# A windowed-attention block on one core: the rows for the MLP are transposed on VectorE and through device memory, not on TensorE; the batch loops get a prefetch hint

## The reference, cut to what matters

```python
xs = jnp.roll(x, shift=(-4, -4), axis=(1, 2))          # then cut into windows of 64 tokens
h = _ln(win, ln1_g, ln1_b)
q, k, v = (einsum('ntc,chd->nthd', h, w) + b for each of the three)
attn = softmax(einsum('nqhd,nkhd->nhqk', q, k) / sqrt(32), axis=-1)
win = win + einsum('nhqk,nkhd->nqhd', attn, v) @ wo + bo
h2 = _ln(win, ln2_g, ln2_b)
win = win + gelu(h2 @ w1 + b1, approximate=False) @ w2 + b2     # w1: 96 x 384, w2: 384 x 96
```

## Time and profile before

| what | value |
|---|---|
| median of three runs | 5434.65 us (5433.81 to 5440.99) |
| the profiled execution | 5443.81 us, its span 5442.0 us |
| busy: PE, DVE, ACT, POOL | 95%, 77%, 69%, 57% of the span |
| mean granted TensorE clock | 0.987 |
| DMA | 208.20 MB on SP's queue, 13.0% of 16 engines |
| device memory | 107.45 MB read, 100.66 MB written |

### The profile page before, as it was taken

How to read it: one execution, slowest core, us unless ns; L and a number is a source line. 1 busy time by engine, 2 the same in 40 slices (tenths; PEclk the granted TensorE clock), 3 DMA queues, 4 the chain that set the end, 5 groups by cost and what they waited for, 6 DMA issues and landing times.

```text
span 5442.0 us, 275140 instructions
## 1 busy us (share of the span) xinstructions
PE 5176.5 (95%) x105172; PEld 4395.4 (81%) x105172; DVE 4179.8 (77%) x9862; ACT 3741.6 (69%) x7758; POOL 3083.7 (57%) x3053
## 2 busy tenths in 40 slices
PE   6999999999999999999999999999999999999999
PEld 4887888878788787888878888788887888878888
DVE  6968768687686877869778697786977869688696
ACT  6839568495784957749477594875938659396693
POOL 5645646466464655646556466464664646556464
PEclk8999999999999999999999999999999999999999
DMA  3011020110201102010120201202011020110201
GB/s 98 3 44 48 27 68 6 47 42 27 68 9 51 36 30 65 11 57 27 33 62 15 61 19 36 59 16 66 13 38 57 19 70 6 41 54 22 73 3 44
DMA packets 92300, 213.96 MB, mean 39 GB/s; under 512 B 22058, under 2 KB 26379, under 8 KB 91851
## 3 DMA queue, kind: packets, MB, share of 16 engines
q1 hardware_dynamic: 91848, 208.20, 13.0%
q10 hardware_dynamic: 2, 0.00, 0.0%
HBM read 107.45 MB, written 100.66 MB: 38 GB/s over the span
## 4 chain that ended last, share of the span: by engine, by line
PE 88%; issue 5%; DVE 5%; SPq 1%; ACT 1%; POOL 0%; DVEq 0%; ACTq 0%; DMA 0%; POOLq 0%
PE psum L585 20%; PE psum L599 19%; PE psum L462 12%; PE psum L430 8%; PE psum L508 6%; PE psum L477 6%; PE psum L494 6%; PE psum L538 5%; PE psum L524 5%; DVE row_max L828 1%; DVE stats L807 1%; DVE stream L857 1%; SPq L251 1%; DVE probs L835 0%; DVE prob_sum L843 0%
## 5 line engine op out<-in xcount | busy, mean ns | idle before, releaser
L297 POOL TENSOR_TENSOR probs<-probs,prob_inv 128x512 f32<-128x512 f32 x771 | 783.1, 1044 | 1496.7 <-DVE prob_inv L851 1496.6
L857 DVE TENSOR_TENSOR stream<-stream,psum 128x384 f32 x1024 | 562.4, 553 | 850.3 <-PE psum L599 760.8
L736 ACT ACTIVATE gelu_odd<-psum 128x512 f32<-128x512 f32 x768 | 459.9, 599 | 732.7 <-PE psum L585 676.9
L736 ACT ACTIVATE gelu_even<-psum 128x512 f32<-128x512 f32 x768 | 459.6, 598 | 682.8 <-PE psum L585 627.1
L376 POOL TENSOR_TENSOR stream<-stream,b_all 128x768 f32 x256 | 493.2, 1931 | 612.4 <-DVE normed L877 584.8
L659 ACT ACTIVATE normed<-stream,shift,rstd 128x96 f32 (+1 forms) x2072 | 770.7, 461 | 43.9 <-POOL shift L345 23.2
L807 DVE BATCH_NORM_STATS2 stats<-stream (+2 forms) x4224 | 725.9, 243 | 57.1 <-DVE stream L857 38.9
L336 POOL TENSOR_TENSOR rstd<-variance,minus_half 128x32 f32<-128x32 f32 (+3 forms) x181 | 747.7, 4131 | 14.2
L304 POOL TENSOR_TENSOR hT<-hT_upper,hT_lower 96x1024 f32<-96x1024 f32 x258 | 613.6, 2378 | 22.8 <-issue 15.6
L828 DVE TENSOR_REDUCE row_max<-psum 128x8 f32<-128x512 f32 x771 | 523.8, 679 | 131.7 <-PE psum L494 116.6
L843 DVE TENSOR_REDUCE prob_sum<-probs 128x8 f32<-128x512 f32 x771 | 497.8, 679 | 109.1 <-ACT probs L693 109.1
(11 more groups left out here) (86 smaller groups left out, 10635.3 us busy)
## 6 DMA issues: line engine op xcount, KB each, us to landing
stream<-in_x SPq DMA_DIRECT2D x272, 192.0 KB
out<-stream SPq DMA_DIRECT2D x256, 192.0 KB
stream<-in_x SPq DMA_DIRECT2D x272, 180.0 KB
out<-stream SPq DMA_DIRECT2D x256, 180.0 KB
stream<-in_x SPq DMA_DIRECT2D x544, 6.0 KB
out<-stream SPq DMA_DIRECT2D x512, 6.0 KB
gelu_odd<-in_L_conv_w SPq DMA_DIRECT2D x1, 144.0 KB
w_w<-in_L_conv_w SPq DMA_DIRECT2D x1, 144.0 KB
```

Source lines behind the costliest of these rows:

```text
L297: nc.gpsimd.tensor_tensor(block_h, block_h, inv, ALU.mult).then_inc(probs_ready, 1)
L736: nc.scalar.activation(gelu[parity][:, j, part * SHARES:(part + 1) * SHARES], psum[:, UP_BANKS[part][j], :], ACT.Gelu).then_inc(gelu_done, 1)
L857: nc.vector.tensor_tensor(part, part, psum[:, banks[g], 0:GROUP], ALU.add).then_inc(added, 1)
```

## The change

**MLP rows.** PE's `transpose2` is gone, and with it the PSUM banks `T2_BANKS`. For each unit DVE does one `nc.vector.transpose` of `normed2` (128 x 768) in blocks of 32 x 32 (`turn_h2`). SP sends the result to a tensor in device memory, `turned_rows`, with three DMAs of 128 KB, one for each block of 32 channels, waits until they have landed, and fetches the unit back as 96 x 1024 with one DMA (`send_turned`, `fetch_turned`). Tokens arrive in another order; ACT's gelu writes its output in an order that undoes it. ACT copies the fetched rows to the upper half in two halves of 512 tokens, DVE subtracts for the first half of the lower, POOL for the second.

**Order of the work.** Units 0, 1 and 2 of a batch are normalised by POOL and turned by DVE during attention; the split of 0 and 1 is POOL's as well, also during attention. The others are turned in the MLP stage, three units ahead; SP sends unit j+4 after it has stored unit j. The buffer of the turned rows is `normed1` (idle in the MLP stage), those of the fetched rows are `probsT` and `oT`. The statistics of the next batch's first three units move from steps 8 to 10 of attention to steps 2 to 4, and POOL's finishing of statistics is spread otherwise, in one more call. PE does both halves of `down` behind both `up`s in every step.

**Loops.** The batch loops of PE, ACT, DVE and POOL (not SP's) get `hint_back_edge=True`: an instruction at the top of the body that names the jump back. PE's loop also gets `head_slot` 0: its first instruction is loaded at the start of a fetch block.

```diff
+        def batches(engine):
+            slots = {engine: 0} if engine == mybir.EngineType.PE else None
+            return nc.Fori(0, BATCHES, engines=(engine,), hint_back_edge=True, head_slot=slots)
...
+            def send_turned(u, source, place):
+                wait_apart(sp, h2_turned, u + 1)
+                for cb in range(CBLOCKS):
+                    sp.dma_start(turned_dram[place, cb].rearrange("c t x -> t c x"),
+                                 source[:, RUN * cb:RUN * (cb + 1)]).then_inc(h2_left, 16)
+
+            def fetch_turned(u, raw, place):
+                wait_apart(sp, h2_left, 16 * CBLOCKS * (u + 1))
+                sp.dma_start(raw, turned_dram[place].rearrange("b c t x -> (b c) (t x)"))\
+                    .then_inc(h2_back[place % 2], 16)
+
+            def fetch_late(u, place):
+                for ready in h2T_ready:
+                    wait_apart(sp, ready, u - 1)
+                fetch_turned(u, raw_late[place % 2], place)
+
             def store_batch(batch_row):
-                with sp.Fori(0, BATCH_ROWS) as r:
+                batch = 2 * batch_row
+                for n in range(2):
+                    send_turned(batch + n, turned_early, n)
+                    fetch_turned(batch + n, raw_early[n], n)
+                send_turned(batch + 2, turned_early, 2)
+                wait_apart(sp, pv_done, batch + BATCH)
+                fetch_turned(batch + 2, raw_late[0], 2)
+                send_turned(batch + 3, turned_late, 3)
+                fetch_late(batch + 3, 3)
+                with sp.Fori(0, 3) as q:
+                    for n in range(RING):
+                        store(batch_row + 2 * q + n // 2, n % 2)
+                        send_turned(batch + 4 * q + n + 4, turned_late, n)
+                        fetch_late(batch + 4 * q + n + 4, n)
+                for row in (6, 7):
                     for half in (0, 1):
-                        store(batch_row + r, half)
+                        store(batch_row + row, half)
...
+            def copy_h2T_lower(b, j, u, parity):
+                second = slice(SHARES, 2 * SHARES)
+                wait_apart(pool, h2T_upper_done, 2 * (BATCH - 2) * b + 2 * (j - 2) + 2)
+                nc.gpsimd.tensor_tensor(h2T[parity][1][0:C, second], raw_late[parity][:, second],
+                                        h2T[parity][0][0:C, second], ALU.subtract).then_inc(h2T_ready[1], 1)
...
-            def transpose2(u, steady):
...
+            def mlp_step(u, parity):
+                up(u, parity, 1, True)
+                up(u + 1, 1 - parity, 0, True)
+                down(u, parity, True)
...
+            def copy_h2T_upper(u, parity):
+                act.wait_ge(h2_back[parity], 8 * (u - parity) + 16)
+                for g in range(2):
+                    tokens = slice(g * SHARES, (g + 1) * SHARES)
+                    nc.scalar.activation(h2T[parity][0][0:C, tokens], raw_late[parity][:, tokens], ACT.Copy)\
+                        .then_inc(h2T_upper_done, 1)
...
+                with act.Fori(0, BATCH // 2 - 1) as k:
+                    for odd in (0, 1):
+                        j = 2 * k + odd
+                        gelus(batch + j, odd, 1)
+                        copy_h2T_upper(batch + j + 2, odd)
+                        gelus(batch + j + 1, 1 - odd, 0)
...
-            def copy_h2T(u, parity):
...
+            def turn_h2(u, turned, first):
+                dve.wait_ge(ln2_ready, u + 1)
+                if not first:
+                    wait_apart(dve, h2_left, 16 * CBLOCKS * u)
+                nc.vector.transpose(turned.rearrange("p (b t i) -> p t b i", b=CBLOCKS, i=BLOCK),
+                                    normed2[:, :, :].rearrange("p t (b i) -> p t b i", i=BLOCK))\
+                    .then_inc(h2_turned, 1)
...
                 def mlp_step(j, parity, row, half):
-                    copy_h2T(batch + j + 1, 1 - parity)
-                    normalise2(batch + j + 2, j + 2)
-                    if row is not None:
-                        statistics1(batch + BATCH + AHEAD + j, AHEAD + j, batch_row + BATCH_ROWS + row, half)
-                    scale2(b, j + 2)
+                    normalise2(batch + j + 3, j + 3)
+                    scale2(b, batch + j + 3, j + 3)
+                    turn_h2(batch + j + 3, turned_late, False)
+                    statistics1(batch + BATCH + AHEAD + j, AHEAD + j, batch_row + BATCH_ROWS + row, half)
+                    copy_h2T_lower(b, j + 2, parity)
                     add_mlp(batch + j)
```

More of the change, by code:

```diff
@@ L57 @@
 LN_OPS = 9
-LN_CALLS = 11
+LN_CALLS = 12
+BLOCK = 32
+CBLOCKS = C // BLOCK
+TBLOCKS = P // BLOCK
+RUN = TILES * BLOCK
+RING = 4
 SPLIT_STEPS = ((0, 0), (1, 0), (0, 1))
@@ L387, in _ @@
             finish1(4, 15, 15, 1)
-            with pool.Fori(0, BATCHES) as b:
+            with batches(mybir.EngineType.Pool) as b:
                 batch = b * BATCH
@@ L568, in attention_step, with up @@
                     project_out(back, 1)
-            def transpose2(u, steady):
-                pe.wait_ge(ln2_ready, u + 1)
+            def up(u, parity, part, steady):
+                pe.wait_ge(h2T_ready[part], u + 1)
                 if steady:
-                    pe.wait_ge(gelu_done, 2 * FCHUNKS * u - FCHUNKS)
-                for g in range(2):
-                    transpose_rows(normed2, T2_BANKS, g, t2_done)
-            def up(u, parity, part, steady):
-                pe.wait_ge(h2T_copied, 2 * u + 1 + part)
-                if part and steady:
-                    pe.wait_ge(gelu_done, 2 * FCHUNKS * u)
+                    wait_apart(pe, gelu_done, 2 * FCHUNKS * u - FCHUNKS * (1 - part))
                 for j in range(FCHUNKS):
-                    if part == 0 and j == 2:
-                        pe.wait_ge(h2T_copied, 2 * u + 2)
                     for step, (w, h) in enumerate(SPLIT_STEPS):
@@ L589, in up @@
                     last.then_inc(up_done, 1)
-            def down(u, parity, part, steady):
-                pe.wait_ge(gelu_done, 2 * FCHUNKS * u + FCHUNKS * (part + 1))
-                if steady:
-                    pe.wait_ge(mlp_added, 2 * u + part)
-                for t in range(TILES // 2):
-                    c = part * (TILES // 2) + t
-                    for j in range(FCHUNKS):
-                        for side in range(2):
-                            last = nc.tensor.matmul(
-                                psum[WT * side:WT * (side + 1), DOWN_BANKS[part], t * C:(t + 1) * C],
-                                gelu[parity][:, j, c * P + WT * side:c * P + WT * (side + 1)], w2_w[:, j, :],
-                                start=(j == 0), stop=(j == FCHUNKS - 1))
-                last.then_inc(down_done, 1)
@@ L605, in mlp_step, with down @@
-            def mlp_step(u, parity, first, last):
-                if not first and not last:
-                    transpose2(u + 1, True)
-                up(u, parity, 1, not first)
-                if first:
-                    transpose2(u + 1, True)
-                    down(u, parity, 0, False)
-                if not last:
-                    up(u + 1, 1 - parity, 0, True)
-                if not first:
-                    down(u, parity, 0, True)
-                down(u, parity, 1, not first)
+            def down(u, parity, steady):
+                pe.wait_ge(gelu_done, 2 * FCHUNKS * (u + 1))
+                for part in range(2):
+                    if steady:
+                        pe.wait_ge(mlp_added, 2 * u + part)
+                    for t in range(TILES // 2):
+                        c = part * (TILES // 2) + t
+                        for j in range(FCHUNKS):
+                            for side in range(2):
+                                last = nc.tensor.matmul(
+                                    psum[WT * side:WT * (side + 1), DOWN_BANKS[part], t * C:(t + 1) * C],
+                                    gelu[parity][:, j, c * P + WT * side:c * P + WT * (side + 1)], w2_w[:, j, :],
+                                    start=(j == 0), stop=(j == FCHUNKS - 1))
+                    last.then_inc(down_done, 1)
@@ L924, in _, with whole_step @@
                 statistics1(n, n, n // 2, n % 2)
-            with dve.Fori(0, BATCHES) as b:
+            with batches(mybir.EngineType.DVE) as b:
                 batch_row = b * BATCH_ROWS
                 batch = b * BATCH
-                with dve.Fori(0, 4) as r:
+                def whole_step(s):
+                    attention_step(batch + s, s % 2)
+                    statistics2(batch + s, s)
+                for s in range(2):
+                    whole_step(s)
+                for n in range(AHEAD):
+                    whole_step(2 + n)
+                    statistics1(batch + BATCH + n, n, batch_row + BATCH_ROWS + n // 2, n % 2)
+                whole_step(5)
+                turn_h2(batch, turned_early, True)
+                whole_step(6)
+                whole_step(7)
+                whole_step(8)
```

(6 more changed lines are left out.)

150 lines of the change are left out of this document (87 added, 63 removed).

## The result

The changed kernel takes **5628.94 us** (median of four runs, 5615.98 to 5631.81) against 5437.03 for the kernel before beside it: a ratio of 1.0345, 95% interval 1.0326 to 1.0363, so 3.45% slower. The forecast was 5410 in a range of 5090 to 5560; sign and range both missed.

A forecast was written before the change was run, and what follows sets the result against it. PE bounds the kernel now; after the change SP bounds the MLP. Per batch +2.8 (MLP) and +0.5 (attention), x16, is +53; the jump back -5.1 x 15 is -77; together -24, so 5434.65 becomes 5410 us, range 5090 to 5560.

The forecast's parts named there:

- SP's time a unit: SP's stores, sends, landing wait and fetch in the MLP: 10.2 us a unit (9.9 to 10.8), against 8.23 for PE.
- sends' round trip: On SP in the MLP: 1.3 us to first bytes, 4.5 moving, 0.1 to the end, for three sends.
- rival (2): SP's sends slower, four engines less than fully used on 1 KB pieces: 8 us for the sends, 6080 us; chance 0.15.
- halfway case: Within rival (2): the sends take 5.5 us, SP 11.2 a unit, the MLP 165, the kernel 5600 us.
- The slack of 3 us: In the MLP, some 3 us of SP's 23.6 us lag a batch is free through ACT's idle time and double buffers.
- The jump back: PE's two gaps at the batch loop's jump, less 1.1 us of a later stop: 5.1 us gained (1.7 to 6.2).
- the first stop: PE standing still for 3.52 us at the batch loop's jump back, which the hint should remove.
- The four engines: SP's three sends in the MLP all use the same four DMA engines, 98.3 KB per engine, 4.2 to 5.1 us.
- The collision: DVE's subtraction against POOL's in the MLP: one a unit, up to 1 us on DVE, still hidden.
- the 17.8 us: MLP gain a batch with PE alone, transposes and first wait gone: 132.7 us against 150.5.
- Rival (1): SP's sends run on 16 engines, the MLP stays at 132.7 to 136: 5095 us (5060 to 5190); chance 0.27.
- Rival (3): At the jump back the hint does nothing: 1.7 instead of 5.1 us a batch, 5460 us; chance 0.08.

The follow-up runs named there:

- spread16_b2: The changed kernel with each unit sent by four DMAs on 16 engines, one per token block, and POOL adding b2 one unit ahead: 5185.48 us.
- before_hint: The kernel before with the hint on the jump back of POOL, PE, ACT and DVE, and no alignment: 5382.5 us, ratio 0.9886.
- spread16: The changed kernel with each unit sent by four DMAs, one per block of 32 token partitions, instead of three: 5334.65 us.
- spread16_b2_tail: spread16_b2 with the last pass of PE's inner MLP loop written out behind the loop: 5125.64 us, ratio 0.9411.
- before_loops: The kernel before with hint and alignment and nothing else of the change: 5380.6 us, ratio 0.9888.
- before_align: The kernel before with the head of PE's loop aligned and no hint: 5425.2 us, ratio 0.9966.

## Why the prediction was wrong, step by step

The forecast gave the profiled execution 5420 us; it took 5631.8, 212 more. Three steps make nearly all of it.

1. **SP's time a unit: 10.2 us forecast, 10.84 measured.** Stores, their waits and the fetch were right (4.3 forecast, 10.84 - 6.62 = 4.2). The term that failed is the sends' round trip: 5.9 forecast, 6.62 measured. In the unit shown above (6.48) the first bytes after 1.3 us were right; moving took 4.8 us, not 4.5; from the last bytes to the end of the wait 0.3, not 0.1, with 0.1 more to the fetch's issue. The rate of an engine was right: 22 slices moved 90 GB/s on average, 22.5 an engine, for 21.8 in the forecast. What 98.3 KB divided by a rate left out is the start, four slices (0.75 us) that moved 18 KB in all. Twelve units of 0.64 us are 7.7 us a batch, 123 us in all. The forecast's upper end for SP, 10.8, all but held it, but its sum stood only 24 us under the old time, which 0.13 us in this term turns round: rival (2) "decides from 4.6 us on" for the sends, and they took 4.8. That rival's halfway case, 5600 us, is near what came, and it had shared a chance of 0.15. I had taken 4.5 from a bracket of 4.2 to 5.1, and let 0.35 of the 0.5 count as faster on the strength of it. The forecast's own upper end was also added up wrongly: 10.8 us a unit gives +10.0 in the MLP, and with 0.5 for attention and 1.7 for the jump 5435 + 16 x 10.5 - 26 = 5577, not 5530. The measured time lies above that too.
2. **The slack of 3 us.** 132.7 + 12 x (10.84 - 8.23) = 164.0, and the stage took 163.97: no slack shows. PE's floor is itself higher, though, by 0.18 us a step (8.41): with it 135.4 + 12 x 2.43 = 164.6, and 0.6 of slack. ACT's idle share was taken for a lead that the fetches could lose. From the last fetch to the end of the stage are 22.2 us in spread16_b2 and 20.6 in the changed kernel, so 1.6 were lost of it, and the first fetch of the stage was 1.0 us later than there: 0.6 net. 3 us x 16 are 48.
3. **The jump back: 5.1 us forecast.** In the whole, stop and attention together, a batch gained 1.9 us (0.47 and 1.44), over 15 jumps 29 instead of 77: 48 us. The step that failed is that the hint removes the first stop. It took off 0.47 us (3.34 to 2.87, where the forecast took off 3.52); the second stop went as forecast (2.45 on average, L494), and the later one grew by about 1.0 (1.43 to 2.43 a jump, L462 to L611), for which 1.1 had been allowed. No row of the kernel before has a hint, so the forecast had nothing to read its effect from; in that kernel it would have been 1.9 (before_hint). Taken apart by runs, the edits' part was 2.1 us in the changed kernel, near the low end of 1.7 to 6.2, and 4.2 in the kernel before. Why the hint does so little in the changed kernel stays open.

123 + 48 + 48 - 8 for attention, which was charged 0.5 us a batch and is counted in the third step, is 211.

**Right.** The four engines: the forecast read them from the closing packets of stores, the sends close with four packets each, the time they took was inside its bracket, and spread16 moved the same bytes at over twice the rate by another cut. That SP would be the bound of the MLP was right as well; the sign was lost in the sizes. The Trainium skill (DMA: Bandwidth & Descriptors, "How many engines (k)") gives the largest number up to 16 that divides both slowest counts, 4 for the kernel's sends and 16 for spread16's; both traces agree, with 4 and 16 closing packets a send. The block transpose: 1.0 us forecast, 0.979 measured. That row and that of the subtraction ahead of it, against the earlier trace rows:

```profile
L961 DVE TENSOR_TENSOR normed<-stream,mean 128x768 f32 x192 | 350.6, 1826 | 51.0 <-issue 48.3
...
L978 DVE STREAM_TRANSPOSE normed<-normed 128x768 f32<-128x768 f32 x208 | 203.6, 979 | 201.4 <-DMA turned_rows<-normed 176.8 <-DVE normed L968 24.5
```

The collision: 1826 ns where the row before had 945, 0.9 us a unit for "up to 1". DVE 6.0 us a unit in the MLP (95.84/16), forecast 6.3 with it; ACT 4.4, forecast 5.1; POOL 6.0, forecast 6.7. All were hidden by SP as said. The fetch landed after 3.3 us, not 2.5, behind SP. The MLP's start: its first matmul had followed attention's end by 2.65 us on average and now follows by 0.28. And the 17.8 us that PE's work alone would give: spread16_b2 has a stage of 136.7 against 150.4, so 13.7; 2.7 of the missing 4.1 are the longer up-projection.

**Rival (1)**, 16 engines, was priced at 5095 (5060 to 5190). The kernel that makes it true took 5334.65. It lacked a step that no term had: POOL's statistics between a lower half and a b2 add. With that step moved it is 5185, inside the price's range at its top: 259 us under the kernel beside it where 338 had been priced. Of the 80 us between, 50 lie in the stage (13.7 us a batch gained, priced at 16.8) and the rest at the jump. **Rival (3)**, that the hint does nothing, was closest on the jump with 1.7 against 2.1 measured, and the first stop is indeed nearly whole. But the hint does work in other code (before_hint, spread16_b2_tail), so its cause was wrong.

So most of the gain that was on offer is real. It went first into four DMA engines, then, behind those, into POOL's order, and part of the loops' gain into a branch that the hint didn't reach. spread16_b2_tail, which mends all three, takes 5125.6 us, 5.9% less than the kernel before and 8.9% less than the changed one; 64 us of the 320 us to the kernel before would be had from hint and alignment alone.

## What to carry to other kernels

Before a transfer goes onto a queue that waits for its landing, work out the number of engines from the outermost counts of both sides, and cut it so that this is 16; if the queue's period is then within a few per cent of the step it must keep up with, give the range, not the sign. Where an engine works in order, look at what stands ahead of the instruction that others wait for, long ones above all: its busy share hides a late add that half the pipeline hangs on. And a wait moved behind other work can cost a whole unit of lead; that has to be written down beside what it hides.

## What the runs showed of the hardware

- **A hinted jump back** took PE 0.4 to 0.5, 1.5 or 3.1 us (medians) by the code around it, an unhinted one 3.6; the alignment was worth 19 us alone in the kernel before, and nothing in spread16_b2. POOL's, ACT's and DVE's own jumps took under 0.1 us, with the hint (before_loops) and without it (before), so all that the loops' edit gives is PE's.
- **A stop costs clock as well.** After the 3.59 us stop shown for before_align the granted clock is at its lower level of 1.2 GHz and the twelve transposes take 2.75 us; after the 1.31 us of before_hint it is at 2.4 GHz and they take 1.46. The granted clock, in the column behind the engines:

```profile
1408.20:1411.00 2.80, 2.80 (x14) 2.80 (x14) 2.66 (x5) 1.20 (x2) 0.00 (x0) 0.50 0.02 6
```

```profile
1394.50:1396.00 1.50, 1.50 (x14) 1.48 (x14) 1.41 (x3) 0.86 (x2) 0.00 (x0) 1.00 0.36 102
```

- **DVE and POOL** hold each other up when both read SBUF: DVE's subtraction and scaling took 2.54 and 3.65 us in the chain of spread16 (0.945 for the pass of the earlier trace rows) beside POOL's b2 adds and the lower half between them, which took 1.92 for 1.28 alone. In the changed kernel 79 of DVE's subtractions began inside a b2 add with nothing of POOL right behind it; each ended 0.82 us after that add did (0.815 to 0.822), and the add took its usual 1.8. The Trainium skill (SBUF — State Buffer, "Who interferes with whom") describes an exclusive lock between a DVE instruction with two SBUF inputs and a GpSimd one that reads SBUF; these times agree with it.
- Issuing a send took SP 0.55 us (median; 0.51 to 0.66) for 128 KB from 128 partitions and 0.43 (most of them 0.31 to 0.45) for 96 KB from 32, so four of the latter cost about as much as three of the former.
